# Attention and feed-forward layer on one core: the second tile's V copied out of PSUM by ScalarE, and new written-out orders for all engines

## The reference, cut to what matters

```
xn  = layernorm(x)                      # x: (8, 256, 128), no weights
a   = layernorm(xn) * ln_w + ln_b
q, k, v = a @ W_q + b_q, a @ W_k + b_k, a @ W_v + b_v     # 16 heads of 64
p   = softmax(causal(q @ k.T / 8))      # 256 x 256 for each batch and head
z   = p @ v
att = sum over heads of z @ W_o + b_o
ffn = relu(xn @ ternary(W1).T + b1) @ ternary(W2).T + b2  # 512 wide
out = x + att + ffn
```

## Time and profile before

| | |
|---|---|
| runs | 227.25, 227.69, 225.07 us; median 227.25 |
| the profiled execution, its own time | 226.65 us |
| span of its profile, first to last instruction | 224.9 us |
| granted clock of TensorE, mean | 1.000 |
| instructions | 9676 |
| busy, us: TensorE, VectorE, ScalarE, GpSimd | 212.5, 202.1, 195.7, 182.5 |

### The profile page before, as it was taken

How to read it: one execution, slowest core, us unless ns; L and a number is a source line. 1 busy time by engine, 2 the same in 40 slices (tenths; PEclk the granted TensorE clock), 3 DMA queues, 4 the chain that set the end, 5 groups by cost and what they waited for, 6 DMA issues and landing times.

```text
span 224.9 us, 9676 instructions
## 1 busy us (share of the span) xinstructions
PE 212.5 (95%) x3670; PEld 187.4 (83%) x3670; DVE 202.1 (90%) x776; ACT 195.7 (87%) x733; POOL 182.5 (81%) x363
## 2 busy tenths in 40 slices
PE   7999799999999999989998999999997999999885
PEld 5666489779997999879997999989986998799674
DVE  3298999999999998999999999999999998899921
ACT  1799999989999889997999889997999799997740
POOL 5569999999979995899959995999959995955630
PEclk9999999999999999999999999999999999999999
DMA  5890538503875658624855658634865748638700
GB/s 149 273 281 6 124 72 219 155 0 59 236 190 136 138 109 208 146 54 111 184 153 136 127 112 217 137 67 111 188 154 126 142 102 207 166 66 210 167 11 23
DMA packets 24030, 30.79 MB, mean 137 GB/s; under 512 B 2608, under 2 KB 23088, under 8 KB 23984
## 3 DMA queue, kind: packets, MB, share of 16 engines
q1 hardware_dynamic: 23840, 30.16, 56.0%
q10 hardware_dynamic: 144, 0.02, 0.0%
HBM read 4.73 MB, written 1.05 MB: 26 GB/s over the span
## 4 chain that ended last, share of the span: by engine, by line
PE 38%; DVE 23%; DMA 11%; ACT 10%; POOL 8%; SPq 4%; issue 3%; POOLq 0%; DVEq 0%
DMA pT<-blocks 11%; DVE s_ps L604 9%; PE m_ps L863 6%; PE s_ps L823 6%; DVE blocks L617 6%; SPq L352 4%; ACT prob L492 3%; PE m_ps L941 3%; ACT prob L494 2%; PE m_ps L788 2%; PE s_ps L734 2%; DVE neg_max L604 2%; PE m_ps L790 2%; PE m_ps L789 2%; DVE zT_lo L623 2%
## 5 line engine op out<-in xcount | busy, mean ns | idle before, releaser
L492 ACT ACTIVATE prob<-s_ps,neg_max 128x256 f32<-128x256 f32 x128 | 65.4, 511 | 2.6 <-DVE neg_max L604 2.3
L315 POOL TENSOR_SCALAR prob<-prob,inv_sum 128x128 f32<-128x128 f32 x126 | 47.1, 374 | 22.1 <-DVE inv_sum L611 21.9
L604 DVE CUSTOM_DVE_ANT_0 s_ps<-s_ps,causal 128x256 f32<-128x256 f32 x128 | 55.8, 436 | 6.8 <-PE s_ps L823 6.5
L316 POOL TENSOR_SCALAR prob<-prob,inv_sum 128x256 f32<-128x256 f32 x126 | 61.3, 486 | 0.0
L617 DVE STREAM_TRANSPOSE blocks<-prob 128x768 f32<-128x768 f32 x62 | 58.8, 960 | 0.7 <-POOL prob L316 0.6
L863 PE MATMUL m_ps<-pT,v 64*64 64x64 f32 (+2 forms) x1536 | 50.0, 257 | 5.9 <-DMA pT<-blocks 3.5
L863 PEld LDWEIGHTS m_ps<-pT,v 64*64 64x64 f32 x1536 | 42.8, 133 | 12.1 <-issue 5.8
L494 ACT ACTIVATE prob<-s_ps,neg_max 128x128 f32<-128x128 f32 x128 | 51.7, 404 | 0.0
L823 PE MATMUL s_ps<-qk 64*64 64x128 f32 (+2 forms) x1280 | 49.7, 275 | 0.8 <-ACT prob L494 0.6
L823 PEld LDWEIGHTS s_ps<-qk 64*64 64x64 f32 x1280 | 42.1, 133 | 5.6 <-issue 3.3
L604 DVE CUSTOM_DVE_ANT_0 s_ps<-s_ps,causal_first 128x128 f32<-128x128 f32 x128 | 42.4, 331 | 0.0
(11 more groups left out here) (120 smaller groups left out, 492.1 us busy)
## 6 DMA issues: line engine op xcount, KB each, us to landing
pT<-blocks SPq DMA_DIRECT2D x124, 192.0 KB, 3.6
xT_cur<-in_xT SPq DMA_DIRECT2D x8, 128.0 KB, 4.6
outT<-out_sb SPq DMA_DIRECT2D x8, 128.0 KB, 4.1
x_all<-in_x SPq DMA_DIRECT2D x1, 768.0 KB, 8.9
wv_raw<-in_w_v SPq DMA_DIRECT2D x2, 256.0 KB, 5.9
...
```

The costliest lines, as they stand in the source:

```text
L315: op(first, first, inv_sum[:, j, 2 + h:3 + h], 0.0, ALU.mult, ALU.add)
L316: last = op(later, later, inv_sum[:, j, h:h + 1], 0.0, ALU.mult, ALU.add)
L492: nc.scalar.activation(later, s_ps[:, pair % 2, h, 0:S].rearrange("p (g j k) -> p g j k", g=TILES, j=QT), ACT.Exp, bias=neg_max[:, j, h:h ...
L604: last = nc.vector.tensor_tensor_reduce(out=sc, in0=sc, in1=mask, scale=-SCALE, scalar=-MASKED, op0=ALU.add, op1=ALU.min, accum_out=neg_ma ...
```

## The change

A new list V_ON_SCALAR = (1, 3) names the steps v1 and v3: those of the second tile of tokens. ScalarE gets a step "v" that copies them with a Copy activation, and raises a semaphore of its own. VectorE's orders have no v1 and v3 any more. TensorE's waits for a copied v, ahead of the reuse of its bank and ahead of stage 0 of duos 0 and 2, ask the semaphore of the engine that copies it. All other steps compute what they did, but the orders of all five engines are new.

```diff
--- before.py
+++ after.py
@@ -23,6 +23,7 @@
 PARTS = [("q", slice(0, 2 * P)), ("k", slice(0, 2 * P)), ("q", slice(2 * P, 4 * P)), ("k", slice(2 * P, 4 * P)),
          ("v", HALF[0]), ("q", HALF[1]), ("k", HALF[1]), ("v", HALF[1])]
 SPLITS = [(name, half) for half in range(2) for name in "qk"] + [("v", 0), ("v", 1)]
+V_ON_SCALAR = (1, 3)
 NBUF = 8
 DUOS = PAIRS // 2
 QB = 32
@@ -46,37 +47,38 @@
 
 
 BUSY = (5, 1)
-PE_HEAD = ("xb:2 pr0:0 pr1:3 xn:2 s0 v0:1 pr2:3 s1 v1:1 pr3:3 s2 pr4:1 ta:0 pr5:2 s3 pr6:3 f0:0 pr7:2 s4 v2:3 "
-           "v3:0 xh+:1 s5 f1:0 xn+:2 s6 pr0+:3 pr1+:0 x0:2 s7 y0:1 z0 s0+ bo:3 pr2+:0 pr3+:3 pr4+:0 x1:2 y1:1 "
-           "s1+ z1 s2+ pr5+:3 v0+:0 pr6+:1 x2:2 y2:3 s3+ z2 v1+:0 s4+ x3:3 y3:2 z3 s5+ v2+:1 v3+:0 pr7+:2 xh++:1 "
-           "s6+ oa:3 f0+:0 f1+:1 s7+ pr0++:0 xn++:2 ob pr1++:1 pr2++:0 pr3++:3")
-PE_PLAN = ("s0 x0-:1 y0-:2 s1 z0- pr4:0 pr5:3 x1-:1 y1-:2 s2 z1- v0:0 pr6:3 x2-:2 y2-:1 s3 z2- s4 pr7:3 v1:0 "
-           "x3-:2 y3-:1 s5 z3- s6 v2:3 v3:0 xh+:2 oa-:1 f0:0 f1:2 s7 pr0+:0 xn+:3 pr1+:2 ob- pr2+:0 pr3+:3")
-PE_TAIL = ("s0 x0-:0 y0-:1 s1 pr4:2 z0- x1-:3 s2 y1-:2 z1- x2-:0 y2-:1 s3 z2- pr5:2 v0:3 s4 pr6:2 v1:3 pr7:0 "
-           "x3-:2 y3-:1 s5 z3- s6 oa-:3 ob- x0:0 y0:1 s7 z0 v2:2 f0:3 x1:0 y1:1 z1 tw6:2 v3:3 x2:1 tw7:0 tn3:2 "
-           "f1:3 y2:0 z2 x3:3 y3:2 z3 oa:1 ob oc")
-ACT_HEAD = ("wh0 wh1 pr0 wh2 xn pr1 wh3 e0 e1 pr2 aa e2 pr3 e3 pr4 pr5 e4 e5 pr6 pr7 f0 e6 e7 xh+ e8 e9 xn+ f1 "
-            "e10 e11 pr0+ e12 e13 e14 e15 pr1+ oh z0 pr2+ e0+ wh4 e1+ pr3+ pr4+ z1 e2+ pr5+ e3+ e4+ e5+ z2 e6+ "
-            "wh5 e7+ pr6+ z3 e8+ e9+ xh++ pr7+ e10+ e11+ e12+ f0+ f1+")
-ACT_PLAN = ("e13- e14- pr0 xn e15- pr1 pr2 pr3 e0 z0- e1 e2 pr4 pr5 z1- e3 e4 e5 pr6 z2- e6 e7 e8 e9 pr7 z3- e10 "
-            "xh+ e11 e12 f0 f1")
-ACT_TAIL = ("e13- pr0 xn e14- pr1 e15- pr2 pr3 e0 e1 pr4 z0- e2 e3 z1- e4 e5 z2- pr5 e6 e7 pr6 e8 e9 pr7 z3- e10 "
-            "e11 e12 e13 z0 e14 e15 f0 z1 w6 w7 f1 z2 z3")
-DVE_HEAD = ("lz nh xb m0 m1 xn v0 ln+ wl0 i0 m2 v1 wl1 m3 m4 m5 th te0 i1 m6 t0 m7 i2 t1 m8 v2 m9 v3 xh+ m10 i3 "
-            "m11 t2 m12 m13 i4 xn+ t3 i5 m14 m15 i6 t4 m0+ t5 i7 t6 bo z0 m1+ t7 ln++ i0+ m2+ m3+ m4+ z1 te1 m5+ "
-            "v0+ m6+ m7+ z2 i1+ v1+ t0+ i2+ m8+ i3+ m9+ z3 v2+ v3+ m10+ m11+ t1+ xh++ m12+ i4+ m13+ t2+ i5+ t3+ "
-            "m14+ m15+ i6+ t4+ o t5+ i7+ xn++ t6+ m0++ m1++")
-DVE_PLAN = ("ln+ m2 z0- m3 i0 t7- m4 m5 z1- t0 i1 v0 m6 m7 z2- m8 m9 t1 i2 v1 m10 m11 i3 z3- v2 m12 i4 v3 xh+ t2 "
-            "t3 i5 m13 m14 m15 i6 t4 t5 xn+ t6 o- i7 m0+ m1+")
-DVE_TAIL = ("t7- m2 m3 i0 z0- m4 m5 i1 z1- t0 m6 m7 v0 i2 z2- t1 m8 i3 m9 v1 t2 m10 t3 i4 m11 z3- m12 i5 t4 m13 "
-            "o- t5 m14 m15 z0 i6 v2 i7 q7 z1 v3 n3 z2 z3 o")
-POOL_HEAD = ("hs np wl2 ln+ p0 p1 p2 wl3 h0 xl+ p3 p4 p5 p6 p7 ol wl4 ln++ p0+ wl5 h1 p1+ p2+ p3+ xl++ p4+ p5+ p6+ "
-             "p7+ h0+ p0++ h1+")
-POOL_PLAN = ("p1 ln+ p2 p3 xl+ p4 p5 p6 h0 p7 p0+ h1")
-POOL_TAIL = ("p1 p2 p3 p4 p5 p6 h0 h1")
-SP_HEAD = ("d0 d1 d2 d3 d0+ d1+ d2+ st")
-SP_PLAN = ("d3- d0 d1 d2 st-")
-SP_TAIL = ("d3- d0 d1 d2 st- st")
+PE_HEAD = ("xb:3 pr0:1 pr1:2 xn:0 pr2:1 s0 v0:3 s1 pr3:0 ta:3 pr4:1 s2 pr5:2 v1:3 s3 v2:3 f0:1 pr6:0 s4 pr7:2 "
+           "f1:3 s5 v3:0 xn+:2 xh+:1 s6 pr0+:3 pr1+:1 s7 pr2+:0 x0:2 y0:3 s0+ z0 bo:1 pr3+:0 s1+ x1:3 y1:2 z1 "
+           "s2+ pr4+:0 pr5+:1 x2:2 y2:3 s3+ z2 v0+:0 pr6+:1 s4+ v1+:0 x3:2 y3:3 z3 s5+ pr7+:1 v2+:0 v3+:2 xh++:3 "
+           "s6+ oa:1 f0+:3 s7+ f1+:2 xn++:0 pr0++:3 ob pr1++:2 pr2++:3 pr3++:0")
+PE_PLAN = ("s0 x0-:2 y0-:1 s1 z0- pr4:3 pr5:0 x1-:2 y1-:1 s2 z1- pr6:3 v0:0 x2-:2 y2-:1 s3 z2- s4 pr7:3 v1:0 "
+           "x3-:2 y3-:1 s5 z3- s6 v2:3 v3:0 xh+:1 oa-:2 f0:3 s7 f1:1 xn+:3 pr0+:0 ob- pr1+:1 pr2+:0 pr3+:3")
+PE_TAIL = ("s0 x0-:0 y0-:1 s1 x1-:2 pr4:3 z0- s2 y1-:3 z1- x2-:1 y2-:0 s3 z2- pr5:3 v0:2 s4 pr6:1 v1:3 pr7:0 "
+           "x3-:2 y3-:1 s5 z3- s6 oa-:3 ob- x0:2 y0:1 s7 z0 v2:0 v3:3 f0:2 x1:1 y1:0 z1 f1:3 tw6:2 x2:1 tw7:3 "
+           "tn3:2 y2:0 x3:2 z2 y3:3 z3 oa:1 ob oc")
+ACT_HEAD = ("wh0 wh1 pr0 wh2 xn pr1 wh3 pr2 aa e0 e1 e2 pr3 e3 pr4 v1 e4 e5 e6 pr5 e7 pr6 pr7 f0 e8 e9 xh+ xn+ f1 "
+            "v3 e10 e11 pr0+ e12 e13 pr1+ e14 e15 pr2+ z0 e0+ e1+ wh4 pr3+ wh5 z1 e2+ e3+ pr4+ e4+ pr5+ e5+ z2 oh "
+            "e6+ e7+ pr6+ z3 v1+ e8+ e9+ pr7+ xh++ e10+ v3+ e11+ e12+ f0+ e13+ f1+ xn++ pr0++ e14+ pr1++ e15+ "
+            "pr2++ pr3++ e0++")
+ACT_PLAN = ("z0- e1 pr4 pr5 e2 z1- e3 e4 e5 pr6 z2- e6 e7 e8 e9 pr7 z3- v1 e10 e11 e12 v3 xh+ f0 e13 e14 xn+ f1 "
+            "pr0+ e15 pr1+ pr2+ pr3+ e0+")
+ACT_TAIL = ("e1 pr4 z0- e2 e3 z1- e4 z2- e5 pr5 e6 e7 pr6 e8 e9 v1 z3- e10 e11 e12 pr7 e13 z0 e14 e15 f0 v3 z1 f1 "
+            "w6 w7 z2 z3")
+DVE_HEAD = ("lz nh xb xn wl0 ln+ m0 v0 m1 m2 th m3 te0 m4 wl1 i0 m5 m6 i1 m7 v2 i2 t0 t1 i3 m8 m9 t2 m10 t3 xh+ "
+            "m11 i4 xn+ m12 m13 ln++ i5 t4 m14 m15 i6 t5 m0+ m1+ i7 z0 t6 m2+ i0+ t7 bo m3+ z1 m4+ te1 m5+ m6+ "
+            "i1+ v0+ m7+ z2 m8+ t0+ m9+ z3 i2+ t1+ i3+ i4+ m10+ m11+ m12+ xh++ v2+ m13+ t2+ t3+ m14+ i5+ t4+ xn++ "
+            "m15+ i6+ t5+ o t6+ i7+ m0++ m1++ m2++ m3++")
+DVE_PLAN = ("z0- t7- ln+ m4 i0 m5 z1- i1 v0 t0 m6 m7 i2 m8 z2- m9 t1 m10 m11 i3 m12 z3- m13 t2 i4 v2 t3 xh+ m14 "
+            "i5 t4 i6 m15 t5 xn+ i7 o- t6 m0+ m1+ m2+ m3+")
+DVE_TAIL = ("t7- i0 z0- m4 m5 i1 z1- m6 t0 z2- m7 t1 i2 v0 i3 m8 m9 t2 m10 t3 i4 m11 z3- m12 i5 m13 t4 o- t5 i6 "
+            "m14 m15 z0 v2 i7 q7 z1 n3 z2 z3 o")
+POOL_HEAD = ("hs np wl2 ln+ p0 p1 p2 p3 h0 xl+ p4 wl3 p5 h1 p6 p7 wl4 wl5 ln++ p0+ p1+ ol p2+ p3+ xl++ p4+ p5+ p6+ "
+             "h0+")
+POOL_PLAN = ("p7- h1- p0 p1 ln+ p2 p3 p4 xl+ p5 p6 h0")
+POOL_TAIL = ("p7- h1- p0 p1 p2 p3 p4 p5 p6 h0 h1")
+SP_HEAD = ("d0 d1 d2 d3 d0+ d1+ d2+ d3+ d0++ st")
+SP_PLAN = ("d1 d2 d3 st- d0+")
+SP_TAIL = ("d1 d2 st- st")
 
 
 def steps(plan, batch):
@@ -225,6 +227,7 @@
         xh_hi = sem("xh_hi")
         xn_hi = sem("xn_hi")
         last_wide = sem("last_wide")
+        v_by_scalar = sem("v_by_scalar")
 
         out_bias_ready = sem("out_bias_ready")
         dve_chain = sem("dve_chain")
@@ -503,6 +506,11 @@
                 wait(act, z_psd, 4 * (DUOS * b + duo + 1))
                 nc.scalar.activation(zT_hi[:, 2 * duo:2 * duo + 2, :], heads_banks(duo, b), ACT.Copy).then_inc(z_hi, 1)
 
+            def values(b, n):
+                half, t = divmod(n, TILES)
+                wait(act, v_psd, 4 * b + n + 1)
+                nc.scalar.activation(v[:, t, HALF[half]], bank("v", n, b), ACT.Copy).then_inc(v_by_scalar, 1)
+
             def hidden(b, n):
                 wait(act, f_psd, 2 * b + n + 1)
                 for half in range(2):
@@ -539,6 +547,8 @@
                     copy_heads(b, index)
                 elif kind == "f":
                     hidden(b, index)
+                elif kind == "v":
+                    values(b, index)
                 elif kind == "xh":
                     heads_input(b)
                 elif kind == "xn":
@@ -736,6 +746,15 @@
             stay_busy(BUSY[0], s_ps[:, 1, 1, 0:S])
             pe.wait_ge(ident_set, 1)
 
+            def wait_values(b, n):
+
+                on_scalar = [k for k in range(4) if k in V_ON_SCALAR]
+                if n in on_scalar:
+                    pe.wait_ge(v_by_scalar, len(on_scalar) * b + on_scalar.index(n) + 1)
+                else:
+                    on_vector = [k for k in range(4) if k not in V_ON_SCALAR]
+                    pe.wait_ge(v_done, len(on_vector) * b + on_vector.index(n) + 1)
+
             def wait_taken(step):
 
                 if BEFORE[step] is None:
@@ -744,7 +763,7 @@
                 if kind == "pr":
                     wait(pe, qk_ready, PAIRS * b + index + 1)
                 elif kind == "v":
-                    wait(pe, v_done, 4 * b + index + 1)
+                    wait_values(b, index)
                 elif kind in "xy":
                     wait(pe, z_lo, PAIRS // 2 * b + index + 1)
                 elif kind == "tw":
@@ -867,7 +886,8 @@
 
                 if stage == 0:
                     if duo % 2 == 0:
-                        wait(pe, v_done, 4 * b + duo + 2)
+                        wait_values(b, duo)
+                        wait_values(b, duo + 1)
                     if by_tensor:
                         pe.wait_ge(last_wide, 2)
                         pe.wait_ge(last_narrow, 1)
```

## The result

The changed kernel takes 228.44 us (median of 12 executions, 227.71 to 229.32). The kernel of before, run beside it on the same chip, takes 226.51 (12 executions, 224.85 to 227.69). The ratio is 1.0095, 95% interval 1.007 to 1.012: slower by about 1%. The prediction was 225.2, slightly faster, with a range up to 228.3. The time lies 0.14 beyond it, and the sign is wrong. The forecast was built on the first three executions of the kernel of before (median 227.25); the median of its 12 is 0.74 lower. Against that base the upper bound would have been 227.6, and the miss 0.9. The profiled execution took 228.54, with a span of 226.6, so it is a typical one.

What follows compares the result with a forecast made beforehand. A TensorE-ScalarE ring of 24.98 us was taken as the floor under periods of 25.24. Middle -0.8, head -0.2 and tail -0.7 gave -1.7 on 226.65, so 224.95, forecast as 225.2; range 221.5 to 228.3.

Steps and rivals of the forecast that it cites:

- Rival 1: Whole kernel: VectorE is the bound and all it loses counts; 219.1 us, or 223 to 221 for half; chance 0.22.
- So in the ring the two copies cost nothing.: Ring B, per batch: ScalarE's waits of 1.4 us hide both copies; without that cover they cost 0.98.
- the wait of v3: TensorE's v3 must wait for ScalarE's copy v1 to free its bank: 0 to 0.1 a batch, taken as 0.05.
- e9: ScalarE's exponential that ends its gapless stretch in Ring B, at 149.58 us; TensorE's next scores follow it.
- Between y3 and s0 the same steps stand as before.: TensorE's order from duo 3's heads to the next scores of pair 0: no matmul added or taken away.
- Ring A: TensorE, VectorE's last transpose and SP's transfers, once around: 25.30 us, to become 24.68 with the statistics' 0.62 moved behind.
- the landings: Duo 3's last transfer, 4.66 us to land, maybe 5.30 with the store ahead of it in time; 0.05 a period taken.
- Ring B: Loop of TensorE and ScalarE from the scores of pair 0 through e9 to the next: 24.98 us, taken as floor.
- The head: Start to the scores of batch 2, VectorE and ScalarE both full: between -2.4 and +2.0 us, taken as -0.2.
- The tail: From the scores of batch 7 to the end, VectorE full: between -1.7 and +1.0 us, taken as -0.7.
- rival 2: Whole kernel: nothing is gained, as late transfers stay or reordered banks cost; 226.6 to 227.3 us; chance 0.13.
- rival 3: Whole kernel: slower, ScalarE becomes the ring with the copies on the path; 232.3 us, half of it 229.5; chance 0.10.

Runs made afterwards that it cites:

- before_narrow: Kernel of before with VectorE's copies v1 and v3 cut from 512 to 8 columns from batch 1 on; 226.51 us, ratio 1.0012.
- new_tail: Kernel of before up to the scores of batch 7, then the changed kernel's order, with copies on ScalarE in batch 7 alone; 226.68 us, ratio 1.0010.
- copies_only: Kernel of before with its orders kept and only v1 and v3 moved from VectorE to ScalarE; 228.0 us, ratio 1.0080.

## Why the prediction was wrong, point by point

**The load.** Right about VectorE. What follows a copy on ScalarE starts 0.47 to 0.48 after it, and the copies take 649 ns in the median (VectorE's in the same kernel 660, and 0.60 from start to start in the earlier trace rows), and VectorE was the busier engine but not the bound: `before_narrow` shows it. Rival 1 (219.1, or half of it, 221 to 223) had 22% and was excluded by a single run. The Trainium skill's rule for it (Perfetto Trace Analysis, Optimizing Scalar/DVE Operations: with VectorE saturated, moving work to ScalarE may make sense) isn't borne out here: at 90% busy its relief of 6 us gave nothing. The other rule of the Trainium skill (ScalarE: Activation LUTs, Rules for kernel authors) names relu, max, min, add and mul, and its figure per element is for bf16. For these fp32 copies out of PSUM the trace doesn't bear it out, as the prediction had said: of the same 512 columns, ScalarE's copy is no slower.

**"So in the ring the two copies cost nothing."** Wrong. Of the two waits of ScalarE that were the cover, one went and the other grew from 2.5 to 3.1 us. The prediction checked only ScalarE's busy sum (24.45 of 24.98). The copies' length costs an estimated 0.7 to 1.0 us in the whole kernel; the wait of v3, put at 0.05 a batch and reasoned at 0 to 0.1, measured 0.26 to 0.37 at the weight load, and 0.10 in the chain. The 0.1 that it allowed for a hand-over is less than the 0.13 from the end of e9 to s6 in the earlier trace rows (149.58, and 149.71 in the same chain).

**"Between y3 and s0 the same steps stand as before."** This is the step that failed worst: the prediction put this stretch at nothing but v3's 0.05, and it grew by 0.42 a period, from 12.87 to 13.29. TensorE's steps are the same, but what they wait for isn't. VectorE's m12 was moved ahead of z3, whose bank xh needs (0.13 in the chain of one period), v3 waits for ScalarE (0.10), and pr1 waits for f1's bank (0.15; bounds were given for it, but no term in the sum). The prediction read VectorE's new order only from s0 to t7. By the medians the swap of m12 and z3 costs 1.1 to 1.2 us of the 1.9 that the kernels lie apart, and it costs in the old kernel too.

**Ring A.** It was named, its 25.30 was read rightly, and the statistics' 0.62 were put at full value: 24.68. The measured ring is 25.61. The transpose did come 0.66 earlier, but from s0 to y3 the mean fell by 0.15 only, since the landing took 5.28, near the upper bound of 5.30. The cause given for that bound, the store behind duo 3, is not it: with the store ahead the landings are as long. And 4.66 was no measure of duo 3: the same trace has 5.06 and 5.19 there, so the 0.05 for the landings went by the lowest of the three that had an undisturbed issue. What makes this transfer take 4.66 once and 5.2 to 5.6 at other times was not found. Ring B's 24.98 was no floor either: `new_tail`, which has the old kernel's orders up to batch 7, has periods of 24.78 (60.23 to 85.01) and 24.83. A ring measured once is one sample of it.

**The head.** Put at -0.2 because both engines were full; it came at +1.26. In copies_only it is +0.8 (61.04), and cutting the copies of batch 1 takes half of that away (60.57). With the new head's orders, s0 of batch 2 came between 61.04 and 61.73 in four other traces with whole copies, and at 61.20 and 61.82 with narrow ones. So the head costs +0.8 to +1.6 by the trace, and cutting the copies takes nothing; which step of the order costs was not found.

**The tail.** -0.7 forecast, -0.9 in the profile; `new_tail` and the spread of the other traces show that such a figure is inside what one execution differs from another. That it hit is luck.

**The cases.** What came lies between rival 2 (up to 227.3) and half of rival 3's price (229.5), and it is rival 3 only partly in mechanism: v3's wait is there, but the greater part is VectorE's order, which no rival had. It got 10%; the forecast got 55%. A sum in which two terms of 0.05 stand for all hand-overs in a ring of four engines was worth less than that.
